# A two-conv residual block in fp32: far rows as 64 by 64 blocks instead of a second 128 by 128 product

## The reference

```python
def _conv3x3(x, w, stride=1):
    return jax.lax.conv_general_dilated(x, w, window_strides=(stride, stride), padding=((1, 1), (1, 1)), ...)
def _bn(x, gamma, beta, mean, var):
    inv = gamma * jax.lax.rsqrt(var + EPS)
    return x * inv[None, :, None, None] + (beta - mean * inv)[None, :, None, None]
identity = x                      # x: (32, 64, 56, 56)
out = jax.nn.relu(_bn(_conv3x3(x, w1, stride=1), g1, b1, m1, v1))
out = _bn(_conv3x3(out, w2, stride=1), g2, b2, m2, v2)
return jax.nn.relu(out + identity)
```

## Time and profile before

| | us |
|---|---|
| median of 3 runs | 566.07 (565.9 to 566.21) |
| the profiled execution, its own time | 565.98 |
| its span, first to last instruction | 564.3 |
| PE busy | 558.4 |
| DVE busy | 542.2 |
| ACT busy | 487.2 |
| granted TensorE clock, as a share of full speed | 1.0 |

### The profile page before, as it was taken

One profiled execution on the slowest core, in us unless ns is written; L12 is line 12 of the kernel. 1 busy time (PEld: TensorE's weight loads), 2 busy tenths in 40 slices (PEclk: granted clock), 3 DMA queues, 4 the chain that ended last, 5 costly groups with the idle time before them and its releaser, 6 DMA issues.

```text
span 564.3 us, 8999 instructions
## 1 busy us (share of the span) xinstructions
PE 558.4 (99%) x3050; PEld 543.6 (96%) x3050; DVE 542.2 (96%) x465; ACT 487.2 (86%) x744; POOL 30.6 (5%) x41
## 2 busy tenths in 40 slices
PE   8999999999999999999999999999999999999997
PEld 4689999999999999999999999999999999999997
DVE  6999999999999999999999999999999999999974
ACT  4789889888889888898888898898898988988876
POOL 3100000000000000000000000000000000000000
PEclk9999999999999999999999999999999999999999
DMA  8655445555435554445554445554355554351013
GB/s 294 180 145 145 151 109 154 148 146 165 155 91 158 159 146 151 136 120 146 174 147 143 126 138 146 149 166 151 97 158 153 146 168 142 102 154 50 30 58 114
DMA packets 31407, 79.20 MB, mean 140 GB/s; under 512 B 2592, under 2 KB 19104, under 8 KB 31392
## 3 DMA queue, kind: packets, MB, share of 16 engines
q1 hardware_dynamic: 26784, 66.05, 32.5%
q0 software_dynamic: 4464, 12.89, 14.6%
q10 hardware_dynamic: 144, 0.07, 0.1%
HBM read 53.31 MB, written 25.69 MB: 140 GB/s over the span
## 4 chain that ended last, share of the span: by engine, by line
PE 96%; DVE 2%; DMA 1%; issue 0%; ACT 0%; SPq 0%
PE psum L702 96%; DMA x_sb<-x_dram 1%; DVE psum L404 0%; DVE x_lo L390 0%; DVE t_outer L358 0%; DVE x_inner L352 0%; DVE x_inner L373 0%; DVE x_inner L354 0%; DVE x_outer L382 0%; DVE w_lo L198 0%; ACT out_sb L603 0%; DVE inv L332 0%; SPq L269 0%; DVE tmp L335 0%; DVE tmp L334 0%
## 5 line engine op out<-in xcount | busy, mean ns | idle before, releaser
L702 PE MATMUL psum<-x_hi,w_hi 128*128 128x420 f32 x488 | 167.2, 343 | 0.7 <-DVE x_lo L390 0.7
L702 PE MATMUL psum<-x_lo,w_hi 128*128 128x420 f32 x488 | 166.1, 340 | 0.0
L702 PE MATMUL psum<-x_hi,w_lo 128*128 128x420 f32 x488 | 166.1, 340 | 0.0
L404 DVE TENSOR_TENSOR psum<-psum,z 128x784 f32<-128x784 f32 (+1 forms) x128 | 126.9, 991 | 4.4 <-ACT z L567 4.3
L573 ACT ACTIVATE hidden<-psum,bias,half_inv 64x56 f32<-64x56 f32 (+2 forms) x128 | 84.5, 686 | 30.8 <-PE psum L702 30.3
L702 PEld LDWEIGHTS psum<-x_hi,w_hi 128*128 128x128 f32 x488 | 91.6, 188 | 2.6 <-issue 1.5
L702 PEld LDWEIGHTS psum<-x_hi,w_lo 128*128 128x128 f32 x488 | 91.7, 188 | 0.5
L702 PEld LDWEIGHTS psum<-x_lo,w_hi 128*128 128x128 f32 x488 | 91.7, 188 | 0.4
L702 PE MATMUL psum<-h_lo,w_hi 128*128 128x392 f32 x256 | 87.3, 341 | 0.0
L702 PE MATMUL psum<-h_hi,w_hi 128*128 128x392 f32 x256 | 87.3, 341 | 0.0
L702 PE MATMUL psum<-h_hi,w_lo 128*128 128x392 f32 x256 | 87.2, 341 | 0.0
(11 more groups left out here) (66 smaller groups left out, 806.3 us busy)
## 6 DMA issues: line engine op xcount, KB each, us to landing
x_sb<-x_dram SPq DMA_DIRECT2D x32, 814.0 KB, 5.0
out_dram<-out_sb SPq DMA_DIRECT2D x63, 392.0 KB, 2.8
x_inner<-x_dram SPq DMA_DIRECT2D x31, 406.0 KB, 3.2
x_inner<-x_dram POOLq DMA_DIRECT2D x31, 406.0 KB, 5.2
out_dram<-out_sb SPq DMA_DIRECT2D x2, 196.0 KB, 2.3
z<-w_dram SPq DMA_DIRECT2D x1, 384.0 KB, 3.7
out_sb<-w_dram SPq DMA_DIRECT2D x1, 384.0 KB, 6.3
bn<-params_dram ACTq DMA_DIRECT2D x1, 68.0 KB, 3.9
```

The source lines that it names most:

```text
L404: nc.vector.tensor_tensor(psum[:, half, EVEN:ODD + 1, 0:width], t1, z[:, half, :, 0:width], ALU.add).then_inc(joined[conv], 1)
L702: ins = nc.tensor.matmul(sums, w[:, i, far, :], t[:, j0:j1, 0:WQ], start=not onto and at == 0, stop=at == len(todo) - 1, skip_group_check= ...
```

## The change

Conv 1's result isn't shifted any more (`NP` is 28). Each product is now one full matmul on the own pair of rows (`pair_products`, L655: three fp32r passes, or one native one) and two native 64 by 64 matmuls for the neighbours' rows (`near_products`, L669), each in one quarter of the array: 64 partitions in, 64 out. Conv 1 leaves the two rows of a pair swapped, so its blocks sit in the two quarters off the diagonal and those of conv 2 in the two on it; `near_rows` issues both in turn. The last line of the host's code swaps the output rows back. Conv 2's inner planes are native altogether, so `ti_hi` and `ti_lo` and their splits are gone. `t_inner`, `t_outer` and `x_outer` are doubled. The residual crosses the halves of the partitions, in instructions of 64 partitions and both banks. ReLU of a half is one instruction instead of two. The lists of DVE and ACT are reordered, and the last image isn't handled by halves in them any more.

```diff
-    NP = NQ + 1
+    NP = NQ
...
-        x_outer = sb("x_outer", [P, 2, RUN])
+        x_outer = sb("x_outer", [P, 2, 2, RUN])
...
-        t_inner = sb("t_inner", [P, 2, NP, WQ])
+        t_inner = sb("t_inner", [P, 2, 2, NP, WQ])
...
-                for i, bank, share in ((0, SUM_T1, 0.5), (1, SUM_T2, -0.5)):
-                    ins = nc.scalar.activation(psum[:, half, bank, 0:width].rearrange("p (j q) -> p j q", q=WQ),
-                                               x_full("inner", k)[0][:, i, j0:j1], ACT.Copy, scale=share)
+                for source, target in ((slice(C, P), slice(0, C)), (slice(0, C), slice(C, P))):
+                    sums = psum[target, half, SUM_T1:SUM_T2 + 1, 0:width].rearrange("p s (j q) -> p s j q", q=WQ)
+                    ins = nc.scalar.activation(sums, x_full("inner", k)[0][source, :, j0:j1], ACT.Copy, scale=0.5)
...
+            def pair_products(conv, half, i, bank, k, native):
+                r0, r1 = HALVES[half]
+                sums = psum[:, half, bank, 0:MAXN].rearrange("p (r q) -> p r q", q=WQ)
+                if native:
+                    passes = ((plane(conv, i, k), wmat[conv][:, i, 0]),)
+                else:
...
+                    passes = ((hi, w_hi[conv][:, i]), (hi, w_lo[conv][:, i]), (lo, w_hi[conv][:, i]))
+                fresh = conv == 1 and i in (1, 2)
+                for at, (t, w) in enumerate(passes):
+                    ins = nc.tensor.matmul(sums, w, t[:, r0:r1, 0:WQ], start=fresh and at == 0,
+                                           stop=at == len(passes) - 1, skip_group_check=True)
...
+            def near_products(conv, half, i, bank, k):
+                r0, r1 = HALVES[half]
+                for source, shift in ((0, 1), (1, -1)):
+                    j0, j1 = max(r0, -shift), min(r1, NQ - shift)
+                    rows = slice(source * C, source * C + C)
+                    place = 1 - source if conv == 1 else source
+                    out = slice(place * C, place * C + C)
+                    sums = psum[out, half, bank, (j0 - r0) * WQ:(j1 - r0) * WQ].rearrange("p (r q) -> p r q", q=WQ)
+                    ins = nc.tensor.matmul(sums, wmat[conv][rows, i, 1, out],
+                                           plane(conv, i, k)[rows, j0 + shift:j1 + shift], start=False, stop=True,
+                                           skip_group_check=True)
...
+            def near_rows(half, of_inner=None, of_outer=None):
+                for i, bank, o, target in ((2, SUM_T2, 0, EVEN), (1, SUM_T1, 3, ODD)):
+                    if of_inner:
+                        conv, k = of_inner
+                        near_products(conv, half, i, bank, k).then_inc(inner[conv], 1)
+                    if of_outer:
+                        conv, k = of_outer
+                        ins = near_products(conv, half, o, target, k)
...
-    found = result.results[0]["out_dram"].reshape(batch, 2, channels, 2, height // 2, width // 2)
+    found = result.results[0]["out_dram"].reshape(batch, 2, channels, 2, height // 2, width // 2)[:, ::-1]
```

More of the change, by code:

```diff
@@ L219, in until, with hidden_outer @@
             return (n - k % 2) * 8 + 16
[L221 to L231, removed]
+        def hidden_outer(b):
+            return t_outer[:, b], h_hi[:, b], h_lo[:, b]
         def split_of_x(which, n):
             return n - 1 if which == "outer" else n
-        def splits(which, n):
-            return n + 1 if which == "outer" else n
         def before_conv2(n):
@@ L405, in join, with sum_hidden @@
                                         ALU.add).then_inc(joined[conv], 1)
[L407 to L414, removed]
+            def sum_hidden(n, b):
+                dve.wait_ge(hidden_ready, 2 * n + 2)
+                wait(dve, inner[2], 4 * (n - 1))
+                nc.vector.tensor_tensor(t_inner[:, b, 0], hid_data[:, 0, :, 0:WQ], hid_data[:, 1, :, 0:WQ],
@@ L415, in sum_hidden, with difference_hidden @@
                                         ALU.add).then_inc(th_ready["t1"], 1)
[L417 to L421, removed]
+            def difference_hidden(n, b):
+                nc.vector.tensor_tensor(t_inner[:, b, 1], hid_data[:, 1, :, 0:WQ], hid_data[:, 0, :, 0:WQ],
                                         ALU.subtract).then_inc(th_ready["t2"], 1)
[L424 to L441, removed]
+            def outer_hidden(n, b):
+                wait(dve, outer[2], 2 * (n - 1))
+                nc.vector.tensor_tensor(t_outer[:, b], hid_cols[:, :, :, 0:WQ],
+                                        hid_cols[:, :, :, 1:WQ + 1], ALU.subtract).then_inc(th_ready["outer"], 1)
@@ L491, in step @@
                     difference_x(s + 1, ka)
-                if last:
-                    sum_hidden(s - 1)
-                    difference_hidden(s - 1)
+                if now:
+                    split_x("outer", s, k)
                 if there_is(s, s - 2):
@@ L653, in step @@
                     copy_sum(2, 0, 1)
+                    high_x("outer", 2, 2)
                     return
-                if now:
-                    high_x("outer", s, k)
-                if last:
-                    high_hidden("t1", s - 1, kl % 2)
+                if ahead:
+                    high_x("inner", s + 1, ka)
+                if there_is(s, s - 2):
+                    relu_out(s - 2, 0)
                 if now:
@@ L676, in step @@
                 if last:
-                    residual(s - 1, kl, 1)
                     copy_sum(2, s - 1, 0)
+                if ahead:
+                    high_x("outer", s + 1, ka)
                 if now:
@@ L747, in outer_products, with inner_pairs_1, outer_pairs @@
+            def inner_pairs_1(half, k, native=False):
+                for i, bank in ((2, SUM_T2), (1, SUM_T1)):
+                    pair_products(1, half, i, bank, k, native)
+            def outer_pairs(conv, n, half, k, native=False):
                 pe.wait_ge(joined[conv], 2 * n + half + 1)
                 for i, bank in ((0, EVEN), (3, ODD)):
-                    first = conv == 1 and (is_step(n, 0) or is_step(n, 1))
-                    passes = whole_passes(1, i, n) if first else passes_of(conv, i, b)
@@ L751, in outer_products, with inner_pairs_2 @@
-                    ins = sum_products(conv, half, i, bank, passes, True)
-                    if conv == 2 and half == 1 and is_step(n, N - 1):
-                        ins.then_inc(last_bank, 1)
-                if not (conv == 2 and half == 1 and is_step(n, N - 1)):
-                    ins.then_inc(outer[conv], 1)
+                    pair_products(conv, half, i, bank, k, native)
+            def inner_pairs_2(n, half, k):
+                pe.wait_ge(th_ready["t1"], n + 1)
+                pe.wait_ge(th_ready["t2"], n + 1)
+                pe.wait_ge(res_ready, 2 * n + half + 1)
+                for i, bank in ((2, SUM_T2), (1, SUM_T1)):
+                    pair_products(2, half, i, bank, k, True)
```

276 lines of the change are left out of this document (112 added, 164 removed).

## The result

The changed kernel takes 561.25 us (median of 4 runs, 561.05 to 561.6), beside 566.0 for the kernel before on the same chip: a ratio of 0.992, 95% interval 0.990 to 0.993. The forecast was 532 with a range of 515 to 575. The time lies inside the range, the direction is right, but the gain is 4.8 us and not 34: the forecast of the size was wrong. By the prediction's own sign it is wrong too: a step is over 16.5.

A forecast was written before the change was run, and what follows sets the result against it. PE was taken to bound the kernel before, at 17.14 us a step, and a chain through ACT and DVE after. Start 32.8, 30 steps of 15.9, end 20.3 and 1.7 outside the span sum to 531.8 us; range 515 to 575.

The forecast's parts named there:

- the prediction's own sign: Stated test: the forecast is wrong if PE is busy without a gap, or a step is over 16.5 us.
- What bounded before: Full steps of the kernel before: PE sets the 17.14 us step, DVE 0.3 us behind, ACT 2.0.
- DVE's load: DVE's work in a full step falls from 16.84 to 14.8 us, busy time to some 480 us.
- ACT's load: ACT's work in a full step falls from 15.14 to 14.0 us, busy time to some 455 us.
- Quarters four at a time: PE's 32 quarter matmuls a step run four together, 5.3 us; one at a time would be 20.3.
- PE's need: PE's work a full step: 14.3 us, or 15.6 if the pipe empties at each of 8 mode changes (1.3).
- Rival 1: Weight loads pace PE's quarters: 7.0 us of quarters, 16.7 a step, 556 us in all; chance 0.14.
- The new chain: One chain round a full step through ACT and DVE: links 15.6 us, 15.8 with handovers, step taken as 15.9.
- The handover from ACT's copies to conv 1's join: Between engines in the chain: each of four handovers costs 0.04 us.
- The residual: ACT's crossed residual, 4 instructions a step: 0.73 us each, 1.46 a pair, at most 0.84 each.
- Start and end: Outside the 30 full steps: start falls from 33.8 to 32.8 us, end rises from 16.3 to 20.3.
- rival 3: Quarters run four at a time, but the order loses more than the chain says: 17.2 a step, 571 us; chance 0.05.

The follow-up runs named there:

- 1: Changed kernel with only the order of ACT's and DVE's lists in the full steps altered; 548.8 us (0.971 of the kernel before).
- 2: Changed kernel with the residual written as before the change, without crossing the partitions (wrong row of a pair added); 534.4 us (0.944).
- 8: Changed kernel with conv 2's inner planes in three fp32r passes again and DVE's second plane moved ahead of `t_outer`; 590.9 us (1.044).
- 10: Changed kernel with its loop of 24 steps written out; 555.2 us (0.981).
- experiment 3: Changed kernel with quarter matmuls of one row of 28 columns instead of 364 or 392; 558.5 us (0.987), a step 16.6.
- 7: On top of 1, ACT does residuals earlier in step 1 and residual of half 1 ahead of `h_hi` near the end; 545.7 us (0.965).
- the loop: On top of 7, the loop written out; 539.5 us (0.954).
- the crossing by DMA: On top of 7 with the loop written out, DMAs write x's inner planes with partition halves exchanged, for ACT's residual to read; 531.6 us (0.940).
- experiment 4: Changed kernel with each group's four quarter matmuls of one conv first, then the other conv's four; 561.4 us (0.992).

## Why the prediction was wrong

- *What bounded before, and DVE's load*: right as far as the rows go; DVE fell to 481.8 us where some 480 were forecast. ACT's load was forecast too low, 455 against 466.5, most of it the residual (0.80 us each and not 0.73).
- *Quarters four at a time*: right, the choice between ends of 5.3 and 20.3 us. PE's need was forecast at 14.3 to 15.6; it is 15.7, and the changes of mode cost a little over the 1.3 taken for emptying the pipe.
- *Rival 1*: wrong. Records start in fours within 0.03 us, so weight loads keep up.
- *"The new chain"* is the step that failed, by its size: "so 15.8 ... a step takes 15.9" was 16.69 in the step shown and 16.68 on average. That a chain through DVE and ACT sets the step is shown: experiments 1, 2, 8 and 10 each move the time in the direction that it says, and 3 leaves the step as it was. Three terms were too small. The handover from ACT's copies to conv 1's join was taken at 0.04, from a pair of instructions with nothing between wait and start; it is 0.20 to 0.33, for register work stands between. The residual was put near its cheap end, 1.46 a pair where it is 1.60. `h_hi` is 0.12 longer. And one stretch was wrong and not only short: `x_hi`, ReLU and copies were taken as the path to the next step, while DVE's own join, `x_inner` and `x_lo` beside them end later. The prediction had DVE's load as a total of 14.8, and never laid its list beside the chain.
- *Start and end*: 53.1 forecast, 59.0 measured. I counted the natives that go at the start and not that with one conv in flight only two quarters are busy, nor the residuals on ACT, for which PE waited 1.19 and 1.42 us there. At the end the late residual was foreseen rightly: PE starts its last inner products 10.0 us after the cut, where 9.7 was forecast. The 1.8 too little lie behind it: to the last store's ReLU at 556.49 it is 9.2 us and not 7.4.
- *The range*: that it holds the time is luck. The forecast's own was 517 to 550; 561 lies in the range only because rivals 1 (556) and 3 (571) were taken in. What happened is nearest to rival 3, the order that loses more than the chain says, to which I gave 0.05; but of its reasons PE's waits for residuals are small, 13.0 us in 38 waits, and experiment 3 shows that PE's part doesn't set the step.
- What I had not weighed at all: that an edit to the order was worth more than all that was left of the change. With 1 alone the forecast's direction would have come with 17 us, with 1, 7, the loop and the crossing by DMA with 34.

## What to carry to other kernels

When a change takes work off every engine, add up the chain that goes round a step before the loads, with the real price of each handover, and lay each engine's own list beside it: where two paths meet, the later one counts. Here the sum was 5% short, more than the chain's distance from PE's load, so a single value for the step was too bold. In an in-order list an instruction is paid by what stands behind it: before moving one, find the next instruction in that list for which another engine waits. And a layout that saves matmuls by exchanging partitions has a bill where the data is needed uncrossed; a DMA can pay it if its queue is half idle.

## What the runs showed of the hardware

- Native matmuls on four different quarters run at full rate together (four records in 0.33 us, as one alone on the whole array), two of them into one bank from different row halves, and start out of the order of the list, by six records at least (experiment 4).
- Going from the whole array to quarters and back costs some 0.35 us for the pair of changes.
- On DVE an instruction starts 0.03 us after the release that it waits for, against a constant or a register alike. With a register instruction and a second wait between, it is 0.20 to 0.33 us.
- ACT takes 0.825 us for 784 elements on 64 partitions (`psum<-x_inner`) and 0.816 on 128 (`out_sb<-psum`).
- In experiment 3, where PE is idle for 104 of the 400 us, in many waits, the mean granted clock of that window is 0.98 of full speed; in the same window of every other kernel here it is 1.00.
